# Moving the constant part of the second feed-forward's updates from VectorE to GpSimd

## What is computed

```python
def _twist(x):
    o_r, o_i, p_r, p_i = jnp.split(x, 4, axis=-1)
    return jnp.concatenate([p_r, -p_i, -o_r, o_i], axis=-1)
global_context = x.mean(axis=1, keepdims=True)
gf = _global_net(global_context, ...)
out = x
for _ in range(3):
    tf = _coupling_net(out, ...)          # four small layers, then a sigmoid: one number per row
    combined = 0.7 * gf + 0.3 * tf
    coupling = 0.1 + adaptive_range * (combined - 0.5) * 2.0
    out = out + coupling * _twist(out)
```

## Time and profile before

| what | value |
|---|---|
| median of three runs | 1379.71 us |
| profiled execution | 1380.12 us |
| its span | 1378.3 us |
| TensorE busy | 95% |
| VectorE busy | 84% |
| ScalarE busy | 76% |
| GpSimd busy | 12% |
| TensorE's granted clock, mean over the span | 0.974 |

### The profile page before, as it was taken

The page is one execution under the profiler, slowest core; times in us unless marked ns, Lnnn a source line. Parts: engine busy times, 40 slices in busy tenths (PEclk is TensorE's granted clock), DMA queues, the critical chain, the costliest instruction groups (busy, mean ns, idle before and its releaser), DMA issues.

```text
span 1378.3 us, 30094 instructions
## 1 busy us (share of the span) xinstructions
PE 1310.4 (95%) x11833; PEld 473.9 (34%) x11896; DVE 1163.7 (84%) x1536; ACT 1054.2 (76%) x2060; POOL 164.8 (12%) x443
## 2 busy tenths in 40 slices
PE   7888999999999898999899999999999999999999
PEld 4343333332333452534233333332333323333533
DVE  6878889999998278555899999999999999995554
ACT  4557888988999546324499999999999999998521
POOL 9234222111111000001000000000000000000000
PEclk9999999999999999899699999999999999999989
DMA  5252301100000012001311000000000000000000
GB/s 147 51 136 40 54 12 36 28 4 12 4 4 4 12 37 56 0 0 52 109 50 49 4 3 12 4 4 3 12 4 3 4 8 9 3 4 3 11 6 25
DMA packets 38524, 35.09 MB, mean 25 GB/s; under 512 B 16080, under 2 KB 31920, under 8 KB 38384
## 3 DMA queue, kind: packets, MB, share of 16 engines
q1 hardware_dynamic: 38384, 33.17, 9.9%
HBM read 17.03 MB, written 9.70 MB: 19 GB/s over the span
## 4 chain that ended last, share of the span: by engine, by line
DVE 32%; PE 21%; issue 1%; ACT 0%; DVEq 0%; ACTq 0%
DVE m_blockmax L1441 31%; PE ps L1323 6%; PE ps L1262 3%; PE ps L1300 3%; PE ps L630 1%; PE ps L619 1%; PE ps L620 1%; PE ps L252 0%; PE ps L245 0%; PE ps L1075 0%; PE ps L1166 0%; PE ps L605 0%; PE ps L648 0%; DVE m_negmax L1449 0%; PE ps L1213 0%
## 5 line engine op out<-in xcount | busy, mean ns | idle before, releaser
L1441 DVE TENSOR_REDUCE m_blockmax<-ps 128x2 f32<-128x1024 f32 (+1 forms) x768 | 880.8, 1207 | 26.6 <-PE ps L1262 18.1
L1414 ACT ACTIVATE m_prob<-ps 128x512 f32<-128x512 f32 (+3 forms) x1664 | 845.9, 577 | 48.0 <-PE ps L1300 33.6
L1300 PE MATMUL ps<-m_q_max,m_k_all 64*128 64x512 bf16 (+3 forms) x1664 | 338.2, 368 | 0.5
L1262 PE MATMUL ps<-m_k_all,m_q_all 64*128 64x512 bf16 (+3 forms) x1664 | 317.8, 380 | 19.9 <-DVE m_blockmax L1441 15.3
L1323 PE MATMUL ps<-m_prob,m_v_op 128*16 128x256 f32 x4096 | 321.0, 385 | 0.1
L1262 PEld LDWEIGHTS ps<-m_k_all,m_q_all 64*128 64x128 bf16 x1664 | 79.8, 93 | 343.2 <-DVE m_blockmax L1441 174.8
L1319 PE MATMUL ps<-m_prob,m_v_op 128*16 128x256 f32 (+3 forms) x2560 | 179.3, 352 | 1.5 <-ACT m_pv L1388 0.8
L1300 PEld LDWEIGHTS ps<-m_q_max,m_k_all 64*128 64x128 bf16 x1664 | 143.3, 94 | 90.5 <-ACT m_prob L1414 47.5
L1323 PEld LDWEIGHTS ps<-m_prob,m_v_op 128*16 128x16 f32 x4096 | 67.4, 94 | 133.5 <-issue 101.3
L1465 POOL CAST m_maxparts<-m_negmax 128x8 bf16<-128x8 f32 x64 | 14.0, 218 | 719.8 <-DVE m_negmax L1449 714.6
L729 ACT ACTIVATE m_prob<-ps 128x512 f32<-128x512 f32 x40 | 23.6, 594 | 74.4 <-PE ps L619 74.4
(11 more groups left out here) (221 smaller groups left out, 1034.8 us busy)
## 6 DMA issues: line engine op xcount, KB each, us to landing
m_part<-m_xn SPq DMA_DIRECT2D x48, 128.0 KB, 2.3
ba_parts<-m_part SPq DMA_DIRECT2D x8, 384.0 KB, 4.7
ea_parts<-m_part SPq DMA_DIRECT2D x8, 384.0 KB, 2.6
m_k_all<-ea_parts SPq DMA_DIRECT2D x84, 32.0 KB
m_q_all<-ea_parts SPq DMA_DIRECT2D x84, 32.0 KB
m_k_all<-ba_parts SPq DMA_DIRECT2D x36, 64.0 KB
m_q_all<-ba_parts SPq DMA_DIRECT2D x36, 64.0 KB
ba_sums<-m_pv SPq DMA_DIRECT2D x128, 9.0 KB
```

The costliest lines, as they stand in the source:

```text
L1262: mm = pe.matmul(ps[:, MX + 2 * (u % 2) + j, 0:width], q_all[head, pair, q0:q0 + TW], k_all[head, pair, CW * kc:CW * kc + width], start=Tr ...
L1300: pe.matmul(ps[:, e % ST, q0:CW], k_all[head, pair, TW * i:TW * i + TW], q_max[m % 2][head, q0:CW], start=True, stop=True).then_inc(self.s ...
L1414: nc.scalar.activation(prob[:, (2 * t + j) % NP, q0:CW], ps[:, e % ST, q0:CW], ACT.Exp, scale=SCALE)\
L1441: nc.vector.tensor_reduce(blockmax[:, m % plan.AHEAD, qt, :, kc], ps[:, MX + 2 * (u % 2):MX + 2 * (u % 2) + 2, 0:width], AX.X, ALU.max)\
```

## The change

For the second use alone (`first` is false), `dve_constant` returns at once, and a new method `pool` runs on GpSimd between the two attentions. For each cycle and chunk it waits for the transfer, multiplies `turned` by c0 into `base`, waits for its own product, and adds `xn` to `base` in place. From the second cycle on it also waits until VectorE has read the chunk's last `base`. Each GpSimd chunk now counts `base_ready` up by two, and `base_count` gives the number that a VectorE sum waits for: i in the first use, 2i - 12 in the second. In `dve_update` VectorE now also waits for the transfer before a step of the second use, since the constant part in front of it did that before. The first use is left as it was.

```diff
--- before.py
+++ after.py
@@ -499,7 +499,26 @@
         dve.wait_ge(self.norm.out, NC * self.ln + c + 1)
         self.nc.vector.tensor_reduce(self.total[:, c:c + 1], chunk(self.xn, c), AX.X, ALU.add).then_inc(self.summed, 1)
 
+    def base_count(self, i):
+        return i if self.first else 2 * i - NC * self.start
+
+    def pool(self, pool):
+        pool.wait_ge(self.scal, 6 * self.use + 6)
+        for s in range(self.start, self.end):
+            for c in range(NC):
+                i = NC * s + c + 1
+                pool.wait_ge(self.turned_in[c], 32 * (s + 1))
+                if s > self.start:
+                    pool.wait_ge(self.updated, i - NC)
+                pool.tensor_scalar(chunk(self.base, c), chunk(self.turned, c), self.c0[:, 0:1], None, ALU.mult)\
+                    .then_inc(self.base_ready, 1)
+                pool.wait_ge(self.base_ready, self.base_count(i) - 1)
+                pool.tensor_tensor(chunk(self.base, c), chunk(self.base, c), chunk(self.xn, c), ALU.add)\
+                    .then_inc(self.base_ready, 1)
+
     def dve_constant(self, dve, s, c):
+        if not self.first:
+            return
         nc = self.nc
         dve.wait_ge(self.turned_in[c], 32 * (s + 1))
         nc.vector.scalar_tensor_tensor(out=chunk(self.base, c), in0=chunk(self.turned, c), scalar=self.c0[:, 0:1],
@@ -507,10 +526,12 @@
 
     def dve_update(self, dve, s, c):
         nc, i = self.nc, NC * s + c + 1
+        if not self.first:
+            dve.wait_ge(self.turned_in[c], 32 * (s + 1))
         dve.wait_ge(self.th_ready, i)
         nc.vector.scalar_tensor_tensor(out=chunk(self.step, c), in0=chunk(self.th, c), scalar=self.c1[:, 0:1],
                                        in1=chunk(self.turned, c), op0=ALU.mult, op1=ALU.mult).then_inc(self.step_ready, 1)
-        dve.wait_ge(self.base_ready, i)
+        dve.wait_ge(self.base_ready, self.base_count(i))
         dve.wait_ge(self.step_ready, i)
         nc.vector.tensor_tensor(chunk(self.xn, c), chunk(self.base, c), chunk(self.step, c), ALU.add).then_inc(self.updated, 1)
         if s == self.end - 1:
@@ -1636,6 +1657,7 @@
                 for c in range(NC):
                     att_b.pool_low(pool, c)
                 att_b.pool_loop(pool)
+                ffn_c.pool(pool)
                 for c in range(NC):
                     att_e.pool_low(pool, c)
                 att_e.pool_loop(pool)
```

## The result

The changed kernel takes 1391.87 us (median of 10 runs, 1384.16 to 1397.55), the one before 1380.37 us (10 runs). The ratio is 1.0085, 95% interval 1.0058 to 1.0111: slower by 11.7 us (8.0 to 15.3). The forecast was 1383.7 us, with a range that ended at 1390.0.

A forecast was written before the change was run, and what follows sets the result against it. VectorE was taken to bound the first cycle, a TensorE-ScalarE chain the later ones; 2.2 + 1.4 + 0.4 = 4.0 us on the profiled 1380.12 gave 1384.1, by the median 1383.7, range 1378.5 to 1390.

The forecast's parts named there:

- The direction and the mechanism: Second feed-forward: slower by 4.0 us, as GpSimd and VectorE reads collide and removing later cycles' constants gains nothing.
- the product's price: GpSimd's one-input product on 512 elements: 0.66 us, taken from a select, with the two-input 1.15 us as upper bound.
- The collision rule: VectorE and GpSimd operations reading SBUF do not overlap; the later one finishes about 0.51 us after the other ends.
- Rival 2: GpSimd's use of the shared path becomes the bound; with a 1.15 us product, 7.7 to 11 us slower; chance 0.19.
- First cycle: 2.65 us a chunk against 2.12; fourth sum 2.8 us later, less 0.66 slack, moves TensorE's multiply by 2.2 us.
- Second and third cycle: VectorE's steps and sums meet GpSimd's work: 1.4 us later in the second cycle, 0.4 us in the third.
- Rival 3: TensorE's clock falls in longer idle times, costing 3.3 us at most; 7.3 with the forecast's 4.0; chance 0.08.
- Rival 1: The two engines run side by side, the third sum ends earlier: -0.8 us, 1378.9; chance 0.08.

The follow-up runs named there:

- e7: Changed kernel with GpSimd's product and sum replaced by one short memset, constant part left out; second feed-forward stage 37.36 us, -0.14 against before, ratio 0.998.
- e3: Changed kernel with GpSimd's product and sum replaced by memsets of about the same length that read nothing; stage 42.37 us, +4.9 against before, ratio 1.0004.
- e9: Changed kernel with GpSimd's product replaced by a plain copy, factor c0 left out; stage 42.89 us, +5.4 against before, ratio 0.9999.
- e5: Kernel before plus 24 extra GpSimd operations in its idle time, to price them; product with a column 1.56 us, with a constant 1.49.
- e6: Changed kernel with the product written as a two-input product with the column broadcast; stage 47.17 us, -2.3 against the changed kernel, ratio to before 1.0073.
- e10: Changed kernel with the product replaced by a memset that reads nothing, the real two-input sum kept; stage 46.17 us, +8.7 against before, ratio 1.0055.
- e4: Changed kernel with dummy multiplies in TensorE's idle time ahead of cycles two and three; stage 47.36 us, -2.1 against the changed kernel, ratio to before 1.0088.
- e11: Changed kernel run once more, unaltered, for a second profile and a closer ratio to before; stage 49.38 us, ratio 1.0076.

## Why the prediction was wrong

**The direction and the mechanism held.** Taking the constants off VectorE won next to nothing (0.14 us in e7); GpSimd's reads and VectorE's made each other wait (none of it is left without the reads, e3); the first cycle lost most. Experiment e9 confirms the working at nearly the price that was put in.

**The step that failed is the product's price.** The prediction had "From above: the two-input 1.15 us" and took a select's 0.66. The price is 1.56, above its upper bound. The 0.66 came from a bf16 select on 24 partitions. The bound rested on the thought that one input can't be dearer than two; e5 shows it can (1.56 against 1.27). With a copy of 0.61 us in its place the stage is +5.4, with the product itself +11.9. The Trainium skill's figure ("GPSIMD Engine Reference", section Performance versus the Vector engine: a port-bound body near 1.03 cycles an element) was further off still as it was read here: 2.5 ns an element is, as an estimate, 3 cycles at the 1.2 GHz of that page's section Specifications. The section on performance gives other rates for bodies with more operations; which of its cases this instruction is, it does not say.

**The collision rule did not hold for the product.** By the rule from the earlier trace rows the step issued at 512.76 beside a product that ended at 514.19 would have ended at about 514.7, 0.51 us behind it; it ended at 513.86. And VectorE's sum at 512.15, issued 0.06 us behind the product, kept its 0.69 us, while the product grew from 1.56 to 2.10. The rule held for copies and two-input operations (e6, e9).

**Rival 2 is what happened in the first cycle.** It had GpSimd as the bound from a product of 0.70 us on. It had 0.19 of the chance, because the margin of 0.2 us a cycle was set against a price never measured. In the later cycles its mechanism is not what the profile shows: GpSimd is busy throughout, but no sum waits for it. By rival 2's own rule, with the measured prices, such a cycle would take 4 x (1.56 + 1.26 + 0.07) + 4.1 = 15.7 us; the second took 14.52 (35.08 less 20.56). So that its 7.7 to 11 us for a product of 1.15 came near 11.9 is in part luck.

**First cycle:** forecast +2.2 at TensorE, measured 6.4 at the next step. GpSimd's length puts the fourth sum 3.7 us later (e3) and its product's reads another 1.7 (e10), together the 5.4. Of these 0.66 is slack, as forecast, and the lower clock adds 1.6 (e4 has 1.5 without it): 3.7 + 1.7 - 0.66 + 1.6 = 6.3.

**Second and third cycle:** forecast 1.4 and 0.4, measured 2.7 and 2.8 (9.1 less 6.4, 11.9 less 9.1). Without reads they cost nothing (e3). In the second, collisions make 2.5 (e4, at full clock). In the third, the last residual is 1.7 later (10.85 less 9.1), and 1.1 are slow multiplies behind it. The last steps and sums meet GpSimd's last products:

```profile
544.17 1.17 DVE L532 SCALAR_TENSOR_TENSOR m_prob<-m_prob,cf_c,m_part 128x512 f32<-128x512 f32 x1 [5.05 <-ACT m_prob L455]
545.45 0.99 DVE L536 TENSOR_TENSOR m_xn<-m_prob 128x512 f32<-128x512 f32 x1
```

GpSimd is done at 548.30. From 548.95 on every sum, step and residual has its old length again.

**Rival 3, the clock,** had 0.08 and was put as an alternative; it came on top, with about 2 us. TensorE's gaps of 1.66 and 2.30 us come from the late sums, so the two could not come apart.

**Rival 1** priced a full success at -0.8 us. e7, whose third sum is 0.28 us earlier, gives -0.14: the third tanh stands close behind VectorE, which the prediction overlooked.

**The range** ended at 1390, below the 1391 of rival 2's own upper end, and rival 2 itself was worked out for no product above 1.15 us.

## What to carry to other kernels

Before work is moved to an engine, measure one instruction of exactly that kind on it: the nearest row, one input and 512 elements, was off by a factor of 2.4, and the bound taken from a two-input row did not hold. Ask what the best case could win (here 0.14 us of 37.5, since the next engine stood right behind) before asking what it may cost. Where two engines share a path, count both engines' turns in a cycle against the period, and treat a margin of a few per cent as none.

## What the runs showed of the hardware that was not expected

- On GpSimd, a 128x512 fp32 product with one tensor input takes 1.49 us (constant) or 1.56 (column), a product with two tensors 1.27, with a broadcast column 1.04, a copy 0.61 (e5).
- The one-input product does not hold VectorE back for its whole length. The step issued at 512.76 beside a product that ended at 514.19 was done at 513.86, before it; in e5 a two-input VectorE operation took 0.82 us when issued 0.41 us into such a product and a plain 0.75 when issued 0.89 us into one. That the product reads only in the first part of its time is an inference from these three cases. Where a copy or a two-input operation held VectorE up, VectorE's operation ended about 0.5 us after GpSimd's (515.07 after 514.52 in e9, 517.67 after 517.13 and 519.35 after 518.80 in e6).
- GpSimd operations that only write (memsets of 1.57, 0.82 and 0.53 us) left VectorE's two-input operations at 0.75 and 0.69 us throughout (e3).
- TensorE's granted clock is part of the price of a late engine, and where it falls differs between profiles of one kernel. Up to the fourth sum, then up to the second cycle's first step, it is 0.85 and 0.79 in one profile of the changed kernel and 0.91 and 0.69 in the other (e11).
